# A LoRA feed-forward block and a mixing layer in fp32r: LoRA of gate and up by two sequences in matmuls of 128 columns, the mixing product in three fp32r products, and the last stores on the sync queue

## The reference, cut to what matters

```python
def _lora_linear(x, W, A, B, adapter_indices):
    base = jnp.einsum('bsd,df->bsf', x, W)
    Ai = A[adapter_indices]
    Bi = B[adapter_indices]
    lora = jnp.einsum('bsr,brf->bsf', jnp.einsum('bsd,bdr->bsr', x, Ai), Bi)
    return base + lora
...
gate = _lora_linear(x, Wg, Ag, Bg, itok)      # 512 -> 2048
up   = _lora_linear(x, Wu, Au, Bu, itok)      # 512 -> 2048
h    = jax.nn.silu(gate) * up
x    = x + _lora_linear(h, Wd, Ad, Bd, itok)  # 2048 -> 512
w    = weights[itok]                          # 64 x 64 each
out  = x + jnp.einsum('bct,bcd->bdt', x, w)   # mixes the 64 tokens
```

## Time and profile before

| what | us |
|---|---|
| median of 3 runs (lowest, highest) | 1329.66 (1327.96, 1330.48) |
| the profiled execution's own time | 1330.62 |
| its span, first to last instruction | 1328.7 |
| PE busy in the span | 1226.5 (92%) |
| PEld busy | 1079.6 (81%) |
| DVE busy | 754.1 (57%) |
| ACT busy | 500.7 (38%) |

### The profile page before, as it was taken

One profiled execution on the slowest core, in us unless ns is written; L12 is line 12 of the kernel. 1 busy time (PEld: TensorE's weight loads), 2 busy tenths in 40 slices (PEclk: granted clock), 3 DMA queues, 4 the chain that ended last, 5 costly groups with the idle time before them and its releaser, 6 DMA issues.

```text
span 1328.7 us, 22783 instructions
## 1 busy us (share of the span) xinstructions
PE 1226.5 (92%) x7072; PEld 1079.6 (81%) x7072; DVE 754.1 (57%) x1341; ACT 500.7 (38%) x951; POOL 96.3 (7%) x190
## 2 busy tenths in 40 slices
PE   3766999989999989999989999989999999999995
PEld 2555778878888878888878888889998999999994
DVE  5434666776666776666776677544334443434341
ACT  3323444454444454444444444443232232322320
POOL 2100110000110000100000000011111111111110
PEclk9778999999999999999989999989999999999998
DMA  3346776567665576665565777375454554455520
GB/s 137 104 145 227 202 211 185 148 196 229 186 168 156 153 206 211 185 176 152 156 201 167 207 209 214 100 235 179 143 149 150 158 162 145 140 156 165 155 62 32
DMA packets 114362, 221.31 MB, mean 167 GB/s; under 512 B 26434, under 2 KB 68546, under 8 KB 114242
## 3 DMA queue, kind: packets, MB, share of 16 engines
q1 hardware_dynamic: 105824, 198.28, 51.2%
q0 software_dynamic: 7552, 19.93, 4.7%
q10 hardware_dynamic: 866, 1.66, 0.3%
HBM read 173.62 MB, written 46.14 MB: 165 GB/s over the span
## 4 chain that ended last, share of the span: by engine, by line
PE 77%; SPq 7%; DVE 5%; issue 4%; ACT 3%; DMA 3%; POOL 0%; ACTq 0%; DVEq 0%
PE ps L856 14%; PE ps L857 14%; PE ps L858 13%; PE ps L868 8%; PE ps L967 5%; PE ps L971 4%; SPq L194 4%; PE ps L975 4%; PE ps L976 4%; PE ps L974 4%; PE ps L969 4%; PE ps L1001 2%; PE ps L885 1%; ACT hh L359 1%; ACT xo_hi L359 1%
## 5 line engine op out<-in xcount | busy, mean ns | idle before, releaser
L856 PE MATMUL ps<-xo_hi,w_hi 128*128 128x512 f32 x896 | 361.2, 403 | 29.0 <-DVE v L657 13.4
L857 PE MATMUL ps<-xo_lo,w_hi 128*128 128x512 f32 x896 | 356.3, 398 | 0.0
L858 PE MATMUL ps<-xo_hi,w_lo 128*128 128x512 f32 x896 | 353.4, 394 | 0.0
L856 PEld LDWEIGHTS ps<-xo_hi,w_hi 128*128 128x128 f32 x896 | 172.2, 192 | 62.0 <-DVE v L657 16.1
L858 PEld LDWEIGHTS ps<-xo_hi,w_lo 128*128 128x128 f32 x896 | 171.2, 191 | 38.4
L868 PEld LDWEIGHTS ps<-t_st,bq 128*128 128x128 f32 x1024 | 158.6, 192 | 53.1 <-DMA bq<-b_dram 32.9
L577 DVE TENSOR_TENSOR hl<-h_raw,hh 128x1024 fp32r<-128x1024 f32 x64 | 78.4, 1226 | 203.1 <-ACT hh L359 203.1
L857 PEld LDWEIGHTS ps<-xo_lo,w_hi 128*128 128x128 f32 x896 | 172.3, 192 | 26.4
L868 PE MATMUL ps<-t_st,bq 128*128 128x256 f32 x1024 | 165.4, 285 | 30.3 <-DMA bq<-b_dram 30.3
L967 PE MATMUL ps<-wd_hl,hh 128*128 128x320 f32 x512 | 167.8, 328 | 6.8 <-DVE hl L577 4.1
L577 DVE TENSOR_TENSOR w_lo<-wsum,w_hi 128x512 fp32r<-128x512 f32 x128 | 88.6, 692 | 145.7 <-ACT w_hi L359 145.7
(11 more groups left out here) (65 smaller groups left out, 1434.9 us busy)
## 6 DMA issues: line engine op xcount, KB each, us to landing
bq<-b_dram SPq DMA_DIRECT2D x1024, 64.0 KB, 2.2
raw<-packed SPq DMA_DIRECT2D x64, 512.0 KB, 5.2
h_dram<-h_f SPq DMA_DIRECT2D x64, 512.0 KB, 3.6
h_raw<-h_dram SPq DMA_DIRECT2D x64, 512.0 KB, 4.0
ad_raw<-a_d SPq DMA_DIRECT2D x64, 128.0 KB, 2.7
xs<-x POOLq DMA_DIRECT2D x16, 512.0 KB, 5.0
y_out_dram<-ys POOLq DMA_DIRECT2D x32, 256.0 KB, 3.3
xst<-xg SPq DMA_DIRECT2D x14, 512.0 KB, 6.3
```

The source lines that it names most:

```text
L856: pe.matmul(bank, st[0], mv[0], start=start and kk == 0, stop=False, skip_group_check=True)
L857: pe.matmul(bank, st[0], mv[1], start=False, stop=False, skip_group_check=True)
L858: m = pe.matmul(bank, st[1], mv[0], start=False, stop=kk == 1, skip_group_check=True)
```

## The change

1. **LoRA of gate and up by two sequences (a "duo").** The 128 rows are now 2 slots x 16 ranks x 2 copies (in pairs of rows) for t x 2 for b hi and b lo, so that one matmul holds all four partial products of a duo. `lora` is four matmuls of 128 columns in place of four of 256. `lora_a` is called for 8 duos in place of 4 quads, with 128 columns, at the ends of the steps 6 to 13. `gather_a` copies two sequences, each value twice.
2. **t.** The two masks act on 512 columns at a time (a "set" of four duos). DVE makes `t_f` and `t_low`, ACT `t_hi`, DVE the sum (`t_sum`, two of 64x512), ACT the copy to the other 64 rows (`t_copy`). This is done at the steps 10 and 14 in place of 5 to 8.
3. **B.** `store_b` issues four transfers (hi and lo, two copies each), and `gather_b` 32 transfers of 32 rows x 2 KB in place of 16 rows x 4 KB.
4. **Mix.** mix and x1 are split in hi and lo, and `mix_tile` is three fp32r matmuls in place of one in fp32. It stands after c = 10. `make_x1` stands in the second batch of the next pair in place of the third.
5. **The end.** In pair 15 the chunks from 4 on run for tile 0 first and then for tile 1. The tail of tile 0 is put between those of tile 1, and the last two stores are issued by SP.

Core of the diff:

```diff
             def store_b(k):
                 sp.wait_ge(b_lo_done, k + 1)
-                sp.dma_start(b_dram[k].rearrange("a r c -> (a r) c"),
-                             b_hl[:, :, :].bitcast(F32).rearrange("p k c -> p (k c)")).then_inc(b_stored, 16)
+                for part in range(2):
+                    for copy in range(2):
+                        sp.dma_start(b_dram[k, part, :, :, copy, :].rearrange("a r (k c) -> (a r) k c", k=PIECE),
+                                     b_hl[:, :, part * WB:(part + 1) * WB].bitcast(F32)).then_inc(b_stored, 16)
...
+            p = PAIRS - 1
+            for j in range(2):
+                sp.wait_ge(y_done, 2 * p + j + 1)
+                sp.dma_start(out[p, :, j], ys[p % 2][:, j, :]).then_inc(y_last_stored, 16)
+            sp.wait_ge(y_last_stored, 32)
...
-                for s in range(QS):
-                    a = number(pool, g * SLOTS + q * QS + s)
-                    pool.tensor_copy(aq[:, :, s, :], a_all[:, bass.ds(a, 1), :, :].rearrange("p a k r -> p (a k) r"))\
-                        .then_inc(a_gathered, 1)
+                for k in range(2):
+                    a = number(pool, g * SLOTS + q * 2 + k)
+                    src = a_all[:, bass.ds(a, 1), :, :].rearrange("p a k r -> p (a k) r")
+                    pool.tensor_copy(aq[:, :, k, :].rearrange("p k (r d) -> p k r d", d=2),
+                                     src.unsqueeze(3).to_broadcast([P, KT * 2, RANK, 2])).then_inc(a_gathered, 1)
...
-            store_y(PAIRS - 1)
             for i in range(2):
-                pool.wait_ge(y_stored[i], 16 * PAIRS)
+                pool.wait_ge(y_stored[i], 32 * ((PAIRS - i) // 2))
...
+            def t_copy(g, b):
+                i = g * SETS + b
+                cols = slice(b * HALF, (b + 1) * HALF)
+                for u in range(2):
+                    act.wait_ge(t_set, 2 * i + u + 1)
+                    t = t_st[u][g % 2]
+                    a, z = (slice(0, 2 * ROWS), slice(2 * ROWS, P))[::1 - 2 * u]
+                    hi(t[z, cols], t[a, cols].bitcast(F32)).then_inc(t_ready, 1)
...
-                if 5 <= c < 9 and g + 1 < GROUPS:
-                    t_mask(g + 1, c - 5)
+                if c in (10, 14) and g + 1 < GROUPS:
+                    t_mask(g + 1, c // 14)
...
                 make_c11(s)
-                if 5 <= c < 9 and g + 1 < GROUPS:
-                    t_lo(g + 1, c - 5)
+                if c in (10, 14) and g + 1 < GROUPS:
+                    t_sum(g + 1, c // 14)
...
-                for part in range(2):
-                    for i in range(2):
-                        q = pair * 2 + i
-                        a = part * WB + u * P
-                        m = pe.matmul(bank[:, i * QT:(i + 1) * QT], b[:, q, c % PIECE, a:a + P],
-                                      t_st[u][g % 2][:, q * QT:(q + 1) * QT], start=start and part == i == 0,
-                                      stop=part == i == 1, skip_group_check=True)
+                for i in range(SD):
+                    q = half * SD + i
+                    m = pe.matmul(bank[:, i * DT:(i + 1) * DT], b[:, q, c % PIECE, u * P:(u + 1) * P],
+                                  t_st[u][g % 2][:, q * DT:(q + 1) * DT], start=start and i == 0,
+                                  stop=i == SD - 1, skip_group_check=True)
...
-                if 4 <= c < 8 and g + 1 < GROUPS:
-                    lora_a(g + 1, c - 4)
+                if 6 <= c < 14 and g + 1 < GROUPS:
+                    lora_a(g + 1, c - 6)
...
-                pe.matmul(ps[2 * (p % 2) + j][:, D:2 * D], mix[p % 2][:, j, :], xs[p % 2][:, j, :],
-                          start=True, stop=True).then_inc(mixed, 1)
+                pe.matmul(bank, mix_hi[p % 2][:, j, :], x1_hi[:, j, :], start=True, stop=False)
+                pe.matmul(bank, mix_lo[p % 2][:, j, :], x1_hi[:, j, :], start=False, stop=False)
+                pe.matmul(bank, mix_hi[p % 2][:, j, :], x1_lo[:, j, :], start=False, stop=True).then_inc(mixed, 1)
...
+            for c in range(BAT, CH):
+                down(p, c, (1,))
+                if c == 8:
+                    turn(p, 0)
+                if c == 11:
+                    lora_down(p, 0)
+            mix_tile(p, 0)
+            turn(p, 1)
+            lora_down(p, 1)
+            mix_tile(p, 1)
```

More of the change, by code:

```diff
@@ L28 @@
 BC = 2 * WB
+ROWS = 2 * RANK
 GATHER = SLOTS * 2 * 16
@@ L191, in gather_b @@
                     a = slot_numbers[b]
[L192 to L195, removed]
+                    for part in range(2):
+                        r = (part * 2 + b % 2) * ROWS
+                        sp.dma_start(bq[n % 2][r:r + ROWS, b // 2, :, :].bitcast(F32).rearrange("r k c -> r (k c)"),
+                                     b_dram[k, part, bass.ds(a, 1)].rearrange("a r d c -> (a r d) c"))\
                             .then_inc(bq_in[n % 4], 16)
@@ L319, in _ @@
             pool.wait_ge(a_in, 16)
-            for q in range(QUADS):
+            for q in range(DUOS):
                 gather_a(0, q)
@@ L323, in _ @@
             gather_a(1, 0)
-            for k in range(2, 6):
+            for k in range(2, PIECES):
                 load_b(k)
[L326 to L332, removed]
+            for g in range(1, GROUPS):
+                for q in range(g == 1, DUOS):
                     gather_a(g, q)
@@ L502, in _ @@
             w_hi_sum(0, 1)
-            for q in range(QUADS):
-                t_hi(0, q)
-                x_hi(0, 3 + q)
-            act.wait_ge(const_in, 48)
+            for b in range(SETS):
+                t_hi(0, b)
+                x_hi(0, 3 + 2 * b)
+                t_copy(0, b)
+                x_hi(0, 4 + 2 * b)
+            act.wait_ge(const_in, 64)
             hi(eye_r[:, :], eye_f[:, :])
@@ L827, in _ @@
                     ad_lo(*divmod(n + 3, BATS))
+                if q == 1 and p:
+                    for j in range(2):
+                        make_x1(p - 1, j)
+                    for j in range(2):
+                        x1_split_lo(p - 1, j)
                 if q == 2:
+                    bd_lo(p)
+                if q == 3:
+                    mix_split_lo(p)
                     if p:
                         for j in range(2):
-                            make_x1(p - 1, j)
-                    bd_lo(p)
-                if q == 3 and p:
-                    for j in range(2):
-                        make_y(p - 1, j)
+                            make_y(p - 1, j)
             p = PAIRS - 1
@@ L958, in down @@
                 first, final = c == 0, c == CH - 1
-                for j in range(2):
+                for j in tiles:
                     tile = ps[2 * (p % 2) + j]
@@ L1025, in _ @@
                         pe.wait_ge(wd_lo_done, c + 1)
-                    down(p, c)
-                    if p and c in (2, 5, 9):
+                    down(p, c, (0,) if last and c >= BAT else (0, 1))
+                    if p and c in (2, 5, 10):
                         for j in range(2):
@@ L1032, in _ @@
                                 lora_down(p - 1, j)
[L1033 removed]
+                            if c == 10:
                                 mix_tile(p - 1, j)
[L1035 to L1040 removed]
+            for c in range(BAT, CH):
[8 more added lines that the diff above has]
+            mix_tile(p, 1)
 def kernel(x, itok_B_0_7, L0_cond_Wg, L0_cond_Wu, L0_cond_Wd, L0_cond_Ag, L0_cond_Bg, L0_cond_Au,
@@ L1060, in by_chunk @@
         return np.asarray(b).reshape(ADAPTERS * RANK, PIECES, PIECE, P)
+    rows = np.arange(P)[:, None]
+    own = rows % (2 * ROWS) // ROWS == np.arange(SLOTS // 2)[None, :] % 2
+    low = rows % 2 == 1
     arrays = {
```

189 lines of the change are left out of this document (111 added, 78 removed).

## The result

The changed kernel takes 1332.74 us (median of 20 runs, 1329.12 to 1335.87) against 1328.89 us of before in the same rounds: a ratio of 1.0024, 95% interval 1.0016 to 1.0033. It is slower by 0.24%; by the medians that is 3.9 us. Its profiled execution took 1333.67 us with a span of 1332.0.

What follows compares the result with a forecast made beforehand. PE was taken to bound the step loop and the second stage, with waits for B's gathers and u3. Terms summed to +2.9 us on 1330.6, so 1333.5; the median lies 0.96 lower, say 1333, range 1316 to 1347.

Steps and rivals of the forecast that it cites:

- The forecast's case: Whole kernel: the summed terms hold, giving 1333 us, alone 1325 to 1342; chance 0.42.
- LoRA matmuls, -5.6: `lora` calls: 0.44 us in place of 0.47, paced by weight loads of 0.11; 5.6 us saved, bounds 0 and 59.
- `lora_a`, +0.6: Groups 2 and 3: eight blocks of 0.9 us, 7.2 against 6.9 before; 0.6 us more for both groups.
- Steps 10 and 14, +8: More DVE masks and sums before u3 stall PE about 1.4 us, six times; 8 us more, bounds 5 and 10.
- the change of group, +1.5: DVE is later when the group changes, lengthening the u3 wait by 0.5 us a change; 1.5 us more (0 to 4).
- Round trips at the start, +7: Group 0: eight POOL and PE rounds of 4.1 us delay the first `lora`; 7 us more, bounds +5 and +9.
- B's way, +11.3: Start, B through DRAM: more stores and register work on SP delay gathers, plus clock loss; 11.3 us more, bounds 4 and 20.
- `lora_a` leaves its cover, +7: Group 0: six blocks from step 8 on lie uncovered, 5.4 us, plus 1.6 for a cold stretch; bounds 4 and 8.
- Mix, -16.8: Second stage: three products per tile and no x1 wait save 1.12 us in 15 pairs; 16.8 us less, bounds 13 and 18.
- The end, -10.1: Tail: POOL's drain lies under PE's work, leaving 10.3 us in place of 20.4; bounds 6 and 12.
- the start costs half: Rival on group 0: the three start terms are 13 us in place of 25, giving 1321 us; chance 0.30.

Runs made afterwards that it cites:

- e5_mix_only: The kernel before with only the mix rewritten into three fp32r products and x1 made earlier, tail and last stores unchanged: 1313.94 us, ratio 0.9885 to before.

## Why the prediction was right

The forecast was 1333 us and the time is 1332.74; the sum was +2.9 and the medians give +3.9. The forecast's case came in, and not by one large miss that another hid: the LoRA half was put at +29.8 and measured +30.0 in the trace (28.2 alone), the second at -26.9 and measured -26.7 (26.2 alone). That the halves fit to 0.2 us is luck. Within the first, the LoRA matmuls saved 3.4 more than put and B's way cost 3.0 more; within the second the mix gave 0.9 less and the end 0.7 more.

- **LoRA matmuls, -5.6: too small.** The mechanism held, as the run with 64 columns and the loads of 96 show: loads set the pace. They start 0.11 apart, as read. But a step gains 0.16, 0.04 a call where the sum had 0.03, and 64 steps 10.2. The discount for 17 steps in which another wait ends last was too large as well. I estimate that only the eight first steps, which end on B, lose it, and 56 x 0.16 = 9.0 is left. The Trainium skill (TensorE: Matmul & The Clock Gate, LDWEIGHTS) has 107 ns for such a load, and the trace's 0.111 agrees. The sustained 81 ns a matmul of 128 columns, which the Trainium skill has on the same page (Back-to-back issue gap), is not reached here.
- **`lora_a`, +0.6.** A block costs 12.25 - 11.36 = 0.89, eight 7.1 against 6.9: +0.2 a group, +0.4 for the two.
- **Steps 10 and 14, +8, and the change of group, +1.5.** Six stalls of 1.43 us are 8.6. The run that takes them away gains 6.4 to 8.1, with 3.2 of new waits in it. The waits of the six old kinds grew by only 22.6 - 8.6 - 13.4 = 0.6.
- **Round trips at the start, +7.** The first `lora` came at 56.54, predicted 56.5 to 57: +6.6.
- **B's way, +11.3: too small.** The `lora` calls that wait for B at steps 2, 4, 6 and 8 are later than before by 3.7, 3.2, 3.4 and 4.0 us more each, 14.3.

  At step 2 it was put at 2.6 and is 3.7. The step that failed there is the store's price: I had three more issues and the old landing, 1.45 together, and it is 3.5 (0.49 each, and 4.6 us to land); against that, the 32 gathers take 0.5 more, not 1.2. At step 4, 3.8 was put and it is 3.2. At the steps 6 and 8, 3.3 and 1.6 for the clock were put, 4.9, and it is 7.4: of the 7.8 that SP's work grew by, I had taken less than half.

  The clock has a part in it too that the sum left out. Behind the wait before step 4 it was 0.50 from 138.3 to 144.0 us, and before the change 0.56 from 124.7 to 128.0. Half of that is lost, some 1.4 us more (an estimate). The waits before steps 6 and 8 were 7.2 and 6.1 us, and the clock behind the first was low, as expected (window from, to, us, PE busy (matmuls), granted clock, DMA share, GB/s):

```profile
171.40:175.00 3.60, 3.60 (x11) 0.50 0.80 223
```

- **`lora_a` leaves its cover, +7.** Six blocks of 0.89 are 5.3, and the clock was 0.50 from 204 to 209 us too, half of which is 2.5: +7.8. With it the terms of the first half add up to 29.3 of the 30.0.
- **Mix, -16.8.** From the first to the last `down` it is 427.2 in place of 443.1 us: -15.9. The mix took 1.37 for the 1.38 predicted, and the idle before it is gone. From the third pair on a pair takes 26.22 in place of 27.34, which is the 1.12 of the forecast; what is missing lies in the first two pairs, 59.8 in place of 61.2. The mix alone gave 15.0 with the old tail.
- **The end, -10.1.** 9.8 us in place of 20.6: -10.8; the chain was put at 10.3. That nearly all of it is the drain shows in the run with the stores alone: -11.0. The rearranged tail adds nothing to that: with the old tail the end came after 8.8 us, and the splits of x1, which that run lacks, cost 1.0 (`e5_mix_only`).

The rival "the start costs half" had named the point from which it decides: a wait before step 6 under 3 us. It was 7.2. But the start was less fixed than the forecast had it: by the runs with the new order on SP, 10.7 us of what the change cost hung on the place of the stores and the loads of x in one queue.

## What to carry to other kernels

Where a run of matmuls each has its own 128x128 weights, count loads, not columns: here 128 and 64 columns took the same time, and going from 256 to 128 gave 0.01 us a matmul, so a layout that halves the columns and keeps the loads pays little. Before transfers are made smaller or more numerous, look at what is issued ahead of the one that is waited for: putting 16 gathers ahead of four stores and of the loads of x gave 19 us, five times what the whole change lost. When a change has halves that touch different stages, time each alone; the sum near zero here hid 26 us.

## What the runs showed of the hardware

- Halving the columns from 128 to 64 behind unchanged loads made a step longer by 0.04 us, not shorter. At full clock loads of 128 columns started 0.11 us apart beside matmuls of 128 or 64 columns, and behind a load of 96 columns the next came after 0.08.
- A gather of the same 64 KB whose source is read twice over costs the SP queue 0.75 to 0.81 us to issue in place of 0.51, while it lands only 0.3 us later.
- POOL's last drain took 9.7 us in the eleven kernels in which SP issued the last stores, and there it began 5 to 9 us before the last matmul of `down`. In the three in which POOL issued them it began after they had landed and took 9.86.
- Stores of 256 KB issued four in a row took 4.6 us each to land (median of 32), where one of 512 KB by itself took 2.7 (median of 8).
